# Fused two-layer image attention on one core: the low part of the third keys tile is computed behind the second query/key split of the next image

## What is computed

```python
def _L0_conv_ref(x, Wq, bq, Wk, bk, Wv, bv, gamma):        # Cq = C // 8 = 32
    q = jnp.einsum('oc,bcn->bno', Wq, xf) + bq
    k = jnp.einsum('oc,bcn->bon', Wk, xf) + bk[None, :, None]
    v = jnp.einsum('oc,bcn->bon', Wv, xf) + bv[None, :, None]
    attn = jax.nn.softmax(jnp.einsum('bnc,bcm->bnm', q, k), axis=-1)
    out = jnp.einsum('bcj,bij->bci', v, attn).reshape(B, C, H, W)
    return gamma[0] * out + x

def _L1_conv_ref(x, norm_w, norm_b, q_w, q_b, k_w, k_b, v_w, v_b, proj_w, proj_b):
    h_ = _group_norm(x, norm_w, norm_b).reshape(B, C, HW)   # 32 groups
    q, k, v = (projections of h_ with 256x256 weights)
    attn = jax.nn.softmax(jnp.einsum('bct,bcs->bts', q, k) * C ** -0.5, axis=-1)
    out = jnp.einsum('bcs,bst->bct', v, attn)
    return x + proj(out)
```

## Time and profile before

| | before |
|---|---|
| median of 3 runs | 804.33 us (803.9 to 804.9) |
| the profiled execution's own time | 804.08 us |
| its span in the trace | 802.3 us |
| granted TensorE clock, mean | 0.995 |
| PE busy | 783.3 us, 98% of the span |
| DVE busy | 550.9 us, 69% |
| ACT busy | 469.2 us, 58% |
| POOL busy | 161.0 us, 20% |

### The profile page before, as it was taken

How to read it: one execution, slowest core, us unless ns; L and a number is a source line. 1 busy time by engine, 2 the same in 40 slices (tenths; PEclk the granted TensorE clock), 3 DMA queues, 4 the chain that set the end, 5 groups by cost and what they waited for, 6 DMA issues and landing times.

```text
span 802.3 us, 9810 instructions
## 1 busy us (share of the span) xinstructions
PE 783.3 (98%) x3816; PEld 646.1 (81%) x3816; DVE 550.9 (69%) x790; ACT 469.2 (58%) x605; POOL 161.0 (20%) x144
## 2 busy tenths in 40 slices
PE   8899989999999999999999999999999999999998
PEld 8687868887888878888788877888788888887886
DVE  5866858778578765787657785676856765575564
ACT  4886556568455775567655586456855565444342
POOL 4800142023100241004210141102310024103300
PEclk9999999999999999999999999999999999999999
DMA  6100010002000110001100011000100010000101
GB/s 184 52 1 1 1 52 1 1 2 105 1 1 1 48 58 1 1 1 53 54 1 1 1 52 53 2 1 0 53 1 1 0 46 8 1 0 1 53 1 52
DMA packets 10365, 18.98 MB, mean 24 GB/s; under 512 B 2128, under 2 KB 3920, under 8 KB 10320
## 3 DMA queue, kind: packets, MB, share of 16 engines
q1 hardware_dynamic: 10320, 18.36, 6.6%
HBM read 9.97 MB, written 8.39 MB: 23 GB/s over the span
## 4 chain that ended last, share of the span: by engine, by line
PE 82%; DVE 11%; ACT 5%; issue 2%; ACTq 0%; POOL 0%; DVEq 0%; POOLq 0%
PE ring L554 25%; PE ring L556 24%; PE ring L555 24%; PE ring L564 4%; PE ring L574 3%; DVE h_lo L919 2%; DVE pt_lo L1024 2%; DVE res L1060 2%; DVE q L985 1%; PE ring L551 1%; ACT prob L773 1%; ACT prob L776 1%; DVE neg_raw L1009 1%; DVE k L977 1%; ACT pt_hi L787 1%
## 5 line engine op out<-in xcount | busy, mean ns | idle before, releaser
L554 PE MATMUL ring<-pt_hi,v_hi 128*128 128x512 f32 x512 | 202.8, 396 | 0.6 <-DVE pt_lo L1027 0.6
L556 PE MATMUL ring<-pt_hi,v_lo 128*128 128x512 f32 x512 | 201.2, 393 | 0.0
L555 PE MATMUL ring<-pt_lo,v_hi 128*128 128x512 f32 x512 | 201.1, 393 | 0.0
L776 ACT ACTIVATE prob<-ring,neg_max 128x1024 f32<-128x1024 f32 x64 | 71.6, 1118 | 160.2 <-DVE neg_max L1010 160.2
L468 POOL TENSOR_TENSOR v_lo<-v_f,v_hi 128x512 fp32r<-128x512 f32 x32 | 43.2, 1351 | 424.7 <-ACT v_hi L814 424.7
L1009 DVE TENSOR_REDUCE neg_raw<-ring 128x1 f32<-128x1024 f32 x64 | 78.3, 1223 | 71.6 <-PE ring L556 71.5
L554 PEld LDWEIGHTS ring<-pt_hi,v_hi 128*128 128x128 f32 x512 | 96.7, 189 | 21.8 <-issue 1.6
L556 PEld LDWEIGHTS ring<-pt_hi,v_lo 128*128 128x128 f32 x512 | 96.6, 189 | 21.3
L555 PEld LDWEIGHTS ring<-pt_lo,v_hi 128*128 128x128 f32 x512 | 96.9, 189 | 19.0
L1024 DVE TENSOR_TENSOR pt_lo<-prob,pt_hi 128x1024 fp32r<-128x1024 f32 x64 | 80.5, 1258 | 35.7 <-ACT pt_hi L787 35.5
L1007 DVE TENSOR_REDUCE neg_max<-ring 128x1 f32<-128x1024 f32 x64 | 77.8, 1222 | 33.7 <-PE ring L564 33.5
(11 more groups left out here) (135 smaller groups left out, 1225.5 us busy)
## 6 DMA issues: line engine op xcount, KB each, us to landing
out_y<-res SPq DMA_DIRECT2D x32, 256.0 KB, 2.2
x_in<-in_x SPq DMA_DIRECT2D x7, 1024.0 KB, 4.8
x_in<-in_x SPq DMA_DIRECT2D x2, 512.0 KB, 5.0
h_f<-in_wv_t SPq DMA_DIRECT2D x1, 256.0 KB, 4.4
res<-in_wq SPq DMA_DIRECT2D x1, 256.0 KB, 7.1
res<-in_wk SPq DMA_DIRECT2D x1, 256.0 KB, 7.3
res<-in_wv SPq DMA_DIRECT2D x1, 256.0 KB, 7.6
res<-in_wp_t SPq DMA_DIRECT2D x1, 256.0 KB, 7.7
```

The lines of the kernel that those rows point to most:

```text
L554: mm(out, w_hi, m_hi, start=first, stop=False)
L555: mm(out, w_hi, m_lo, start=False, stop=False)
L556: return mm(out, w_lo, m_hi, start=False, stop=last)
L776: activation(prob[:, p % PROBS], ring[:, slot], ACT.Exp, bias=neg_max[:, k % 2:k % 2 + 1], accum_out=row_sum[:, k % 2:k % 2 + 1]).then_inc ...
```

## The change

A step gets a flag `low_later`, set for step 2 of the turns with a next image (i = 2 to 6). In such a step DVE does not call `prob_lo` for the step's keys tile. The tile is kept in `postponed`, and the next step calls `prob_lo` for it behind the query/key split and in front of its own keys tile.

```diff
-        self.take_weights = self.opening = self.rest = self.low_first = False
+        self.take_weights = self.opening = self.rest = self.low_first = self.low_later = False
...
         steps[3].sides = tiles("qk", i + 1, (1,))
+        steps[2].low_later = True
...
-            pending = None
+            pending = postponed = None
...
                 for entry in first:
                     if entry[0] != "norm":
                         follow(entry)
+                if postponed:
+                    prob_lo(postponed)
+                postponed = now.tile if now.low_later else None
                 if now.evacuate_at_once:
                     evacuate(*now.evacuate_at_once)
...
-                elif now.tile and not now.low_first:
+                elif now.tile and not now.low_first and not now.low_later:
                     follow(now.tile)
```

## The result

| | before | changed |
|---|---|---|
| median | 804.58 us (803.9 to 805.18, 8 runs) | 807.09 us (806.38 to 807.88, 8 runs) |
| ratio to before | | 1.003 (95% interval 1.0021 to 1.0039) |
| span of the profiled execution | 802.3 us | 804.7 us |
| PE waiting for `q` of the second split | 3.3 us, 6 places | 0.7 us, 1 place |
| PE waiting for the low part of a keys tile | none | 4.3 us, 5 places |

The change makes the kernel 2.5 us slower. The forecast was 806.3 us, 804.0 to 807.2.

The account below looks back on a forecast made before the run. PE, busy 98% of the span, was taken to bound the kernel. Losses of 0.44 + 3 x 0.47 + 0.11 = 1.96 us on 804.08 gave 806.04, plus 0.25 for the median: 806.3 us, range 804.0 to 807.2.

Parts of the forecast that it names:

- The wait for `q`: PE's scores tile 0 waits for DVE's `q`: 3.3 us in six places, 2.5 us of it in turns 2 to 6.
- ACT as the second bound: Turn 3: `q` also waits for ACT's part, ending at 284.69 and not moving, so `q` gains only 0.58 us.
- mark: Old start of the low part of keys tile 2, from which times are counted: 282.51 in turn 3, 186.59 in turn 2.
- The low part's arrival: On DVE, the moved low part starts 0.77 us behind the start of `q`, at 285.49 in turn 3.
- The collision: The moved low part waits for a POOL copy in progress; in turn 3 PE's second values matmul comes 0.47 us later.
- The cover: ACT's `query_hi` waited 0.86 us for PE, hiding a row maximum about 1.0 us later; costed at nothing.
- The reserve behind it: Even with `query_hi` late by some tenths, PE first needs that slot and those values about two us later.
- The size: Losses at PE's second values matmul in turns 2 to 6: 0.44 + 3 x 0.47 + 0.11 = 1.96 us.
- The unknown: Landing of stores releasing POOL: before the mark 0.47 (0.44) us, a little behind 0.9, well behind 0.1 to 0.3.
- The wash: Rival: DVE wins the port and POOL's copies do not get in the way; -0.14 us, 804.2; chance 0.25.
- The faster case: Rival: PE's wait goes and nothing replaces it, needing `q` 0.39 us earlier; -2.5 us, 801.8; chance 0.06.
- The slower-by-more case: Rival: stores land just behind the mark in most turns, so L461 holds the low part; 4.5 us, 808.8; chance 0.07.

## Why the prediction was right

- **The wait for `q`** goes in exactly the five turns (3.3 us in six places to 0.7 in one). ACT as the second bound held: its half runs 381.03 to 381.71, and `q` starts 0.03 us later, at +2.21, as worked out (284.72 against a mark of 282.51).
- **The low part's arrival** at +2.98 and, in turn 2, at +2.73 (worked out +2.71).
- **The collision** is the cause, and it is shown, not only argued: with the copies out of the way and VectorE's order left as changed, the loss goes; the same move in the kernel before does nothing. The forecast of 1.07 us from the copy's end to the low part's end came out at 1.07.
- **The cover** behind it held. The row maximum is 1.07 us later (+5.78 for +4.71), and `query_hi` still waits 0.41 us for PE, of 0.86 before. PE shows no new wait there or at keys tile 5. The reserve behind it was misread, though: "PE first needs that slot and those values about two us later" is not so. In turn 3 before the change `query_lo` ends at 292.97 and PE's scores tile 1 starts at 293.03, and when `query_hi` was late by 0.33 us in a turn of the run with ScalarE's half early, PE waited 0.31.
- **The size** was short: 1.96 us forecast, 2.28 measured at the five places, 2.5 in the medians. Two terms of the sum were mis-sized. "The first L453 is held by `h_lo` alone and ends at 281.38 + 2.20": in turn 4 it is the second `h_lo`'s start plus 2.3, since I had taken the 2.20 from a copy held by a low part; that shifts the `x` copy from +2.37 to +2.45. "PE starts 0.06 us behind the end": that row was of an odd tile, with one wait, and here it is 0.15. Less 0.04 for the matmul behind it, these make 0.13 us in turns 4 and 5, 0.47 to 0.60, and in turn 2, 0.44 to 0.57.
- **The unknown** was rightly named, and its price for late landings was too low. Turn 3's stores landed at +1.07 instead of -0.14, so its low part met the second `res` copy and lost 0.40; turn 6 stayed at about +0.8 and cost 0.12 for 0.11, but in the second profile of the changed kernel it landed at +1.36 and cost 0.69. The prediction gave "0.1 to 0.3" to all of these. Its own working for turn 6, carried on to landings at +1.07 and +1.36, gives 0.37 and 0.66 us.
- **Luck.** 807.09 lies 0.11 us inside the upper bound of 807.2, and the second set of the changed kernel, 807.41, above it. The mechanism was right; that the median fell inside the range is partly luck. The medians of the kernel before alone differ by 0.3 us from set to set (804.39 to 804.69), and how late the stores land, on which up to 0.7 us a turn depends, changes from one execution to the next.
- **The rivals.** The wash is what the kernel does without the collision (1.0005). The faster case had its condition right (ScalarE's half 0.39 us sooner), but that is not enough: it also takes the copies out of the way, or a start within a tenth of theirs. The slower-by-more case needed landings just behind the mark, which no profiled turn had; the dearest turn seen, 0.69 us, came by a later one.

## What to carry to other kernels

An instruction's place in its queue also sets whom it meets at a shared port. Before moving a VectorE instruction with two SBUF operands, look at what GpSimd does at the new time, and re-time GpSimd as well, since the instruction may have been what held it back. And if a wait is bound by two queues at nearly the same time, moving one of them gains nothing: here three edits that were each worth nothing or less (1.003 for VectorE's order, 0.9999 for ScalarE's, 1.0001 for GpSimd's) gave 0.9971 together.

## What the runs showed of the hardware

- Of a VectorE instruction with two SBUF operands and a GpSimd copy, the one that the trace shows to start first does not always win. VectorE went first, undisturbed, when it started up to 0.12 us behind the copy (0.01, 0.06, 0.10, and 0.12 in the run with halves, at 113.63); 0.15 and 0.28 us behind, it waited for the copy and ended 1.07 us behind the copy's end. The Trainium skill, "SBUF — State Buffer", section "SBUF: two separate sides", gives the pair to whichever starts first: the trace agrees from 0.15 us on and differs below.
- A VectorE instruction that waits mostly goes in front of GpSimd's next copy, and a second one right behind it does too (the copy at 383.16 took 3.21 us). Neither is a rule. With ScalarE's half early, a `res` copy at 284.04 (2.24 us) got in between two low parts in turn 3, and the second took 2.06 us. With the copies in halves, a low part waiting since 33.42 was passed by a half (to 33.97) and by the cast behind it (33.92 to 34.53), and took 2.18 us. What decides is open.
- PE started 0.15 us behind what it waited for when another, long-met wait was written in front of that one, and 0.05 us behind with the order reversed.
